# Cross attention on one Trainium2 core: the stabilizer's rows reach the query stack by transfers through DRAM instead of by turns on TensorE and copies

## What is computed

```
q, k, v = heads(x_q @ wq), heads(ctx @ wk), heads(ctx @ wv)
scores = q @ k.T / sqrt(16) + mask_or_relative_bias
probs = softmax(scores)            # over 4096 keys
out = probs @ v
```

## Time and profile before

| | us |
|---|---|
| three runs | 1622.54, 1625.29, 1626.94 |
| median | 1625.29 |
| the profiled execution | 1628.63 |
| its span, first to last instruction | 1626.8 |
| one head of cross attention, start to start | 11.1 |
| heads in all | 64 |

### The profile page before, as it was taken

How to read it: one execution, slowest core, us unless ns; L and a number is a source line. 1 busy time by engine, 2 the same in 40 slices (tenths; PEclk the granted TensorE clock), 3 DMA queues, 4 the chain that set the end, 5 groups by cost and what they waited for, 6 DMA issues and landing times. The chain is left out here.

```text
span 1626.8 us, 36711 instructions
## 1 busy us (share of the span) xinstructions
PE 1534.0 (94%) x12495; PEld 916.9 (56%) x12509; DVE 1057.2 (65%) x1619; ACT 874.6 (54%) x1910; POOL 338.7 (21%) x623
## 2 busy tenths in 40 slices
PE   9999998999999997998989999879999999989596
PEld 4444443444444444674868999724444444446396
DVE  6777788888888854748553111278888888726511
ACT  3222225888888883742632111238888888856232
POOL 1412221111111111020202444141111111100153
PEclk9999999999999999999989999999999999999799
DMA  6587763554554547100048999845545545222074
GB/s 213 178 209 233 217 177 82 90 90 77 90 88 77 91 93 183 35 1 1 2 146 272 327 315 318 262 80 95 93 78 87 89 79 88 48 24 83 29 231 131
DMA packets 158311, 207.46 MB, mean 128 GB/s; under 512 B 32135, under 2 KB 130434, under 8 KB 151158
## 3 DMA queue, kind: packets, MB, share of 16 engines
q1 hardware_dynamic: 149429, 199.99, 49.1%
q0 software_dynamic: 6720, 4.31, 1.6%
q10 hardware_dynamic: 2064, 1.87, 0.4%
HBM read 165.95 MB, written 41.39 MB: 127 GB/s over the span
## 5 line engine op out<-in xcount | busy, mean ns | idle before, releaser
L1339 DVE TENSOR_REDUCE top<-ps 128x1 f32<-128x1024 f32 x504 | 588.5, 1218 | 95.5 <-PE ps L1172 95.4
L1303 ACT ACTIVATE probs<-ps 128x512 f32<-128x512 f32 x1024 | 557.6, 601 | 132.1 <-PE ps L1204 121.4
L1204 PE MATMUL ps<-qst,kst 128*128 128x256 bf16 x2048 | 317.6, 276 | 4.8 <-ACT probs L1303 3.5
L1218 PE MATMUL ps_o<-probs,vst 128*32 128x256 f32 x4096 | 274.9, 386 | 1.4 <-ACT probs L1303 1.4
L1204 PEld LDWEIGHTS ps<-qst,kst 128*128 128x128 bf16 x2048 | 158.0, 98 | 205.8 <-ACT probs L1303 162.6
L1172 PE MATMUL ps<-kst,qst 64*128 64x512 bf16 (+1 forms) x519 | 170.6, 387 | 11.2 <-DVE top L1339 6.1
L1218 PEld LDWEIGHTS ps_o<-probs,vst 128*32 128x32 f32 x4096 | 107.0, 109 | 99.9 <-issue 41.5
L1172 PE MATMUL ps<-kst,q1st 64*128 64x512 bf16 x488 | 160.6, 386 | 0.0
L402 POOL COPY vst<-vall 128x512 f32 (+1 forms) x64 | 39.1, 611 | 555.3 <-PE ps_o L1218 552.2
L2437 PE MATMUL ps_h<-xe,vall 128*128 128x80 f32 x1024 | 149.7, 265 | 0.0
L2437 PEld LDWEIGHTS ps_h<-xe,vall 128*128 128x128 f32 x1024 | 136.3, 191 | 0.1
(11 more groups left out here) (458 smaller groups left out, 2126.7 us busy)
## 6 DMA issues: line engine op xcount, KB each, us to landing
kst<-kd SPq DMA_DIRECT2D x372, 128.0 KB
kd<-probs SPq DMA_DIRECT2D x64, 384.0 KB, 3.0
vall<-in_L_ffn_wg_dram SPq DMA_DIRECT2D x32, 512.0 KB
vall<-in_L_ffn_wu_dram SPq DMA_DIRECT2D x32, 512.0 KB
vall<-in_L_ffn_wd_dram SPq DMA_DIRECT2D x32, 512.0 KB
w<-in_L_ffn_w_dram SPq DMA_DIRECT2D x16, 1024.0 KB
vd<-square_weights SPq DMA_DIRECT2D x16, 512.0 KB, 4.1
vall<-vd SPq DMA_DIRECT2D x16, 512.0 KB, 6.5
```

Source lines behind the costliest of these rows:

```text
L1204: mm = pe.matmul(ps2[:, scores[u], x, :], kst[:, m, kt * P:(kt + 1) * P], qst[:, m, :], start=True, stop=True)
L1218: mm = pe.matmul(ps_o[32 * j:32 * j + 32, :], vst[:, b, kt, :], probs[:, (kt // 2) % SLOTS, kt % 2, :], start=(kt < 4), stop=(kt >= KT - 4 ...
L1303: nc.scalar.activation(probs[:, u % SLOTS, :, :], ps2[:, scores[u], :, :], ACT.Exp).then_inc(probs_ready, 1)
L1339: v.tensor_reduce(top[:, b, qt, c:c + 1], ps1[:, u % 2, :], AX, ALU.max).then_inc(mx, 1)
```

## The change

The columns of `cp` are no longer turned on TensorE, except for head 0 of each layer. For heads 1 to 31 SP stores the three columns, number by number (two transfers of 128 x 3 numbers of 2 bytes), as rows of a small DRAM tensor, waits until they have landed, and loads the three rows of 512 bytes into the query stack. GpSimd waits, before it overwrites `cp`, until the stores of the head before have landed. Unit 0 of pass 2 waits for the load (`c_in`). SP's list for head g becomes: second query rows, key rows, then the rows of head g - 2.

```diff
+    pr.c_dram = nc.dram_tensor("c_dram", [NBUF, NPIECE, S], BF16, kind="Internal").ap()
...
+        c_in = [pr.sem(st, f"c_in{m}") for m in range(NBUF)]
+        c_stored = [pr.sem(st, f"c_stored{m}") for m in range(NBUF)]
...
             def _(sp):
+                def turned_rows(n, m):
+
+                    wait_at(pr, sp, c_steps, C_STEPS * n)
+                    if not (isinstance(n, int) and n < FIRST):
+                        wait_at(pr, sp, q_ready, n + 1 - FIRST)
+                    else:
+                        sp.wait_ge(q_first[1], 2)
+                    for qt in range(QT):
+                        sp.dma_start(pr.c_dram[m, :, qt * P:(qt + 1) * P].rearrange("k p -> p k"), cp[:, qt, 0:NPIECE],
+                                     allow_slow_non_contiguous=True).then_inc(c_stored[m], 16)
+                    wait_at(pr, sp, c_stored[m], 8 * (n - m) + (32 if m >= 1 else 0))
+                    sp.dma_start(qst[CROW:CROW + NPIECE, m, :], pr.c_dram[m]).then_inc(c_in[m], 16)
...
                 for c in range(1, C):
                     sp.wait_ge(buffers.q_in[c], 16 * len(Q_ROWS))
+                turned_rows(1, 1)
                 with sp.Fori(1, NG // NBUF) as h2:
                     for m in range(NBUF):
                         g, h, _, b = head_number(h2, m)
                         wait_at(pr, sp, sc2, N2 * (g - NBUF + 1))
                         buffers.second_q(sp, h, m, b)
                         buffers.keys.load_k(sp, buffers.L, h, m)
+                        turned_rows(g - 2, (m + 2) % NBUF)
+                for m in range(2, NBUF):
+                    turned_rows(NG - NBUF + m, m)
...
-                def c_rows(n):
+                def c_rows(n, m):
 
                     pool.wait_ge(c_max, n)
+                    if not (isinstance(n, int) and n == 1):
+                        before = (m - 1) % NBUF
+                        pool.wait_ge(c_stored[before], 8 * (n - 1 - before) + (32 if before >= 1 else 0))
...
-                    if u == 0:
-                        pe.wait_ge(c_ready, g + 1)
+                    if u == 0 and first:
+                        pe.wait_ge(c_ready, 1)
+                    elif u == 0:
+                        pe.wait_ge(c_in[m], 4 * (g - m) + (16 if m >= 1 else 0))
                     if u == TURN_AT + 2 and not first:
                         pe.wait_ge(raw_ready, g)
-                    elif u == TURN_AT + 3 and not first and not last:
-                        pe.wait_ge(c_ready, g + 2)
...
-                        if u == (FIRST_TURN_AT if first else TURN_AT) and not last:
-                            turn_c(g + 1, place)
...
-                        if u == (FIRST_TURN_AT if place == "first" else TURN_AT) and place != "last":
-                            copy_c(g + 1, (m + 1) % NBUF, ps_first_c if place == "first" else ps_c)
```

More of the change, by code:

```diff
@@ L984, in cross_attention @@
     FIRST_SCORES2 = tuple((u + 2 * (u > FIRST_TURN_AT)) % 3 for u in range(N2))
-    F_SLOT, C_SLOT, FIRST_C_SLOT = (TURN_AT + 1) % 3, (TURN_AT + 2) % 3, (FIRST_TURN_AT + 2) % 3
+    F_SLOT, C_SLOT = (TURN_AT + 1) % 3, (TURN_AT + 2) % 3
     C_STEPS = 4
@@ L1000, in cross_attention @@
         ps_c = ps2[:, C_SLOT, 0, 0:P].bitcast(BF16)
-        ps_first_c = ps2[:, FIRST_C_SLOT, 0, 0:P].bitcast(BF16)
         ps_f = ps2[:, F_SLOT, 1, 0:QT * 64].rearrange("p (t d) -> p t d", t=QT)
@@ L1135, in _ @@
                 copy_first_v(1)
-                c_rows(1)
+                c_rows(1, 1)
                 for c in range(1, C):
@@ L1144, in _ @@
                         copy_q(g, h, m, m % 2)
-                        c_rows(g - 2)
+                        c_rows(g - 2, (m + 2) % NBUF)
                 for m in range(2, NBUF):
                     copy_v(*head_number(NG // NBUF - 1, m))
-                    c_rows(NG - NBUF + m)
+                    c_rows(NG - NBUF + m, m)
             @block.tensor
@@ L1174, in pass1, with turn_first_c @@
                     mm.then_inc(sc1, 1)
[L1176 to L1183, removed]
+                def turn_first_c():
+                    pe.wait_ge(c_first, CHAIN)
                     for qt in range(QT):
-                        mm = pe.transpose(turned[:, qt * P:(qt + 1) * P], cp[:, qt, :], pr.cb("identb"))
+                        mm = pe.transpose(ps_c[:, qt * P:(qt + 1) * P], cp[:, qt, :], pr.cb("identb"))
                     mm.then_inc(c_turned, 1)
                 def pass2(g, m, b, u, place):
-                    first, last = place == "first", place == "last"
+                    first = place == "first"
                     scores = FIRST_SCORES2 if first else SCORES2
-                    if u == 0:
-                        pe.wait_ge(c_ready, g + 1)
+                    if u == 0 and first:
+                        pe.wait_ge(c_ready, 1)
+                    elif u == 0:
+                        pe.wait_ge(c_in[m], 4 * (g - m) + (16 if m >= 1 else 0))
                     if u == TURN_AT + 2 and not first:
                         pe.wait_ge(raw_ready, g)
-                    elif u == TURN_AT + 3 and not first and not last:
-                        pe.wait_ge(c_ready, g + 2)
                     elif u == (FIRST_TURN_AT if first else TURN_AT) + 1:
@@ L1277, in _ @@
                     pe.wait_ge(q_read, C)
-                    turn_c(0, "before")
+                    turn_first_c()
                 else:
-                    turn_c(0, "before")
+                    turn_first_c()
                     for u in range(2):
@@ L1291, in copy_o, with copy_first_c @@
                     nc.scalar.copy(o_sb[:, b, :], ps_o).then_inc(o_copied, 1)
-                def copy_c(g, m, turned):
-                    act.wait_ge(c_turned, g + 1)
-                    nc.scalar.copy(qst[CROW:CROW + NPIECE, m, :], turned[0:NPIECE, :]).then_inc(c_ready, 1)
+                def copy_first_c():
+                    act.wait_ge(c_turned, 1)
+                    nc.scalar.copy(qst[CROW:CROW + NPIECE, 0, :], ps_c[0:NPIECE, :]).then_inc(c_ready, 1)
                 def head(g, h, m, b, place):
@@ L1327, in _ @@
                         act.wait_ge(buffers.k_out[q], 16 * NB)
-                copy_c(0, 0, ps_c)
+                copy_first_c()
                 all_heads(act, head)
```

## The result

The kernel after takes 2487.3 us, median of four runs (2482.81 to 2491.06); the kernel before took 1623.91 (1621.10 to 1626.94) beside it. The ratio is 1.532, 95% interval 1.530 to 1.535: 863 us more, where 36 were forecast and 1730 was the upper end of the range.

A forecast was written before the change was run, and what follows sets the result against it. TensorE, busy 94%, was taken to set the pace. Head stalls 30.8, less 4.8 gain, plus 7.9 in layer 1's head 1 and 2.0 for the clock: 35.9 us on 1625.3, forecast 1661, range 1622 to 1730.

The forecast's parts named there:

- the turns' 0.08 us per head: Unit 8 of a head, without turns: 0.08 of 0.20 us gained, 4.8 us over 60 places (0 to 12.0).
- T + 5.2: Issue of a head's first store, counted from T, when SP starts its work for a head; 5.2 us later.
- heads lose in pairs: Heads 2 to 29, both layers: two in a row lose 1.1 us together, 0.55 each, 30.8 us over 56.
- The chain as a whole: Stores, landing and row load before unit 0: rows land at T + 11.9, due at T + 10.8.
- where I had 2.0: Row load of three 512-byte rows: 2.0 us to land, the shortest landing shown; bounds 1.0 and 3.5.
- I take 1.0 us behind the key loads, T + 9.7: Stores' landing in each head: key loads end at T + 8.7, then 0.4 us of packets and 0.6 for landing.
- My upper bound, 3.5 us: Stores' landing at most 3.5 us behind the key loads, T + 12.2, taken from the mask's store.
- The third rival: Slow 2-byte stores in every head: rows at T + 13.5 to 14, +111 us, 1736 (1682 to 1790); chance 0.20.
- A head then takes 4.7 + (L - 5.2): For rows landing at T + L with a stall over 0.8 us, a head loses L - 11.6 against 11.1.
- I had allowed for it once, in layer 1: Lowered granted clock behind the stall at layer 1's head 1: 2 us added (0 to 4).
- Layer 1's head 1: SP waits there for the last query rows, so the stabilizer rows come 7.9 us late, once (6.3 to 10.9).
- its 2.0 + 2.0: Layer 1's head 1: 2.0 us for the stores' landing and 2.0 for the row load's.

The follow-up runs named there:

- the run with two hops: Changed kernel storing whole 64 bytes, then loading three rows of zeros from an input; stabilizer zero, exponential scale 0.1: 1664.2 us against 1622.2, ratio 1.026.
- the series: Landings of the store variants by writes into one 64 bytes, from 1.99 us (one whole 64-byte write) to 15.1 and 16.6 (32 writes).

## Why the prediction was wrong, point by point

**Right.** That TensorE sets the pace and that only the turns' 0.08 us per head come back: 4.1 (1.5 to 6.7) measured for 4.8. GpSimd's last step and SP's list as the two things that come before the store: T + 5.2 against T + 5.6 in the run with two hops. That key loads ahead of the stores delay their landing: with stores of 64 bytes it takes 10.4 - 5.6 = 4.8 us behind the key loads, and 2.0 with nothing ahead. That heads lose in pairs. The chain as a whole: +36 for +42 when the landing costs about what I had taken, with some luck: the row load was issued 0.5 us later than forecast, and from its issue to unit 0 it took 1.4 us where I had 2.0. About 48,000 more packets under 512 bytes: 81921 less 32135 on the page of before, 49,786.

**Wrong, and it decided: the step "I take 1.0 us behind the key loads, T + 9.7".** I put the landing together from 48 packets of 8.5 ns and 0.6 us. The packets do take that: the window from 714 to 716 shows 0.4 us of them. The landing, from the first issue, is 15.1 us in the median, and as long with nothing ahead in the queue. In layer 0's head 1 the window before the store shows the DMA engines at 0.00; SP's timeline stands under it:

```profile
264.00:265.80 1.80, 1.45 (x11) 0.49 (x10) 1.76 (x4) 1.57 (x3) 0.80 (x4) 1.00 0.00 0
```

```profile
265.83 0.92 SPq L1048 DMA_DIRECT2D c_dram<-cp  x2
281.35 0.26 SPq L1051 DMA_DIRECT2D qst<-c_dram  x1
```

My upper bound, 3.5 us, was taken from a store of the same number of pieces, but pieces of 128 bytes, each whole in itself. It was "the nearest row by its count of pieces", and the series says that the count of pieces is what doesn't matter. No row bounded what the change does: 2-byte writes side by side, 32 to each 64 bytes. The row load was priced too low as well, 3.0 us for 2.0; the load of three rows in the run with two hops took 1.4, and why the one from `c_dram` takes 1.6 more wasn't tried.

**The third rival** is the one that the result belongs to, by the sign set out for it, a head over 12.2 us with a late landing. It named the right fact, that many 2-byte stores go "to the same few hundred bytes, from all 16 engines", and priced it wrongly: 50 ns for each of 48 packets, 2.4 us, from which 1736 and at most 1790. Measured, 12.7 us are added to a landing (15.1 - 2.40). A price per packet was the wrong form: the packets are as short as ever, and 256 writes land no sooner than 768. The Trainium skill, DMA: Bandwidth & Descriptors, section Specifications, has the read-modify-write below 512 bytes as its rule. The runs bear on it from both sides: 768 writes of 2 bytes land in 2.40 us when apart, against 1.99 for 256 of 64 bytes, which are under 512 too, so being smaller still costs little; 32 of them in the same 64 bytes cost 15.1. That each must there read what the one before has left would explain both, but no run looked inside the memory.

**The formula for a large landing was right in form and lacked a term.** "A head then takes 4.7 + (L - 5.2)": landing and row load in it give 4.7 + 15.15 + 3.04 = 22.9 us; 24.9 were measured. The missing 2 us are the clock: I had allowed for it once, in layer 1, and not in a stalled head, since the heads were to stall by a microsecond. They stall by ten; the clock falls to 0.50 in each, and unit 0 to the end of GpSimd's last step takes 6.6 us for 4.6. At 0.8 and 0.99 us of stall, with the two hops, unit 0's matmuls keep their 0.39 us. With it the account closes: 62 heads wait for their rows; 62 x (22.9 - 11.1) = 732, 62 x 2.0 = 124, less 4 of gain, is 852 of the 863. Windows of the two cross attentions, in the columns of before:

```profile
252.00:1040.00 788.00, 422.39 (x3640) 175.44 (x3644) 298.52 (x299) 288.14 (x569) 53.21 (x184) 0.74 0.24 38
1495.00:2300.00 805.00, 426.97 (x3657) 177.88 (x3660) 305.93 (x304) 288.65 (x570) 63.24 (x199) 0.75 0.24 37
```

Before, these stretches lasted 364.5 and 368.0 us with PE busy for 358.4 and 358.7; PE's busy time grows by 64 and 68, with some hundred instructions fewer: the clock, which falls from 0.99 to 0.74 and 0.75.

**Layer 1's head 1**, forecast 7.9 us late (6.3 to 10.9): with the two hops its unit 0 has waited for 5.25 us, under my bounds; in the changed kernel 19.83 us. SP's timeline, then TensorE's, of the changed kernel:

```profile
1526.49 0.92 SPq L1048 DMA_DIRECT2D c_dram<-cp  x2
1541.13 0.27 SPq L1051 DMA_DIRECT2D qst<-c_dram  x1
```

```profile
1543.93 0.61 PE L1221 MATMUL ps<-qst,kst 128*128 128x256 bf16 x2 [19.83 <-DMA qst<-c_dram]
```

Store to row load 14.6, row load to unit 0 2.8: the terms of every other head. The place was right, its 2.0 + 2.0 were not.

**The chances.** I gave slower 0.70 and the slow stores 0.20 with an end at 1790. The direction held; the range ended where my price for a packet ended. The one thing that the trace could not price stood in the kernel's longest possible place, in front of every head, and I bounded it by rows that lacked its peculiarity.

**Open.** Whether the count of writes in 64 bytes decides or how many of the 16 engines meet there; what the unit is, between 16 and 512 bytes; whether single numbers into an SBUF row are slow as neighbours or for the one partition; what stops TensorE and ScalarE, beside the keys, while such stores are under way. A version that beats the kernel before isn't in sight of these runs: with the turns gone at no cost at all there were 4 us to win.

## What to carry to other kernels

A column that is to become a row through small transfers costs by its neighbours, not by its packets: when a store writes 2 bytes here and its neighbours go to the same 64 bytes, expect some 15 us from issue to landing, and other loads of the core held up meanwhile. Whole 64 bytes, or numbers spread apart, land in 2.0 to 2.5 us, but the single numbers then have to be gathered into the row, which took 8.2; no run here made the row cheaply. Two turns and a copy on engines with room are worth 0.07 us a head (4.1 us at 60 places), and a DRAM round trip in front of every head must fit into the slack of the chain or it is paid in full, with the clock on top. And when the trace lacks the operation itself, choose the nearest row by where its bytes go and not by their count, and leave the upper end open where none is near.

## What the runs showed of the hardware that I had not expected

- Stores whose packets are over by 716, with the DMA engines at 0.00 from there, land 12 us later. The packet rows don't show the price.
- 768 writes of 2 bytes: landing 2.40 us at 64 bytes' distance, 2.6 at 32, 4.35 at 8, 15.1 side by side. A write of 64 bytes in place of 32 writes of 2: 1.99.
- Such stores hold up others: with them TensorE waits 199 us for keys that it had not waited for before, and 198 when the stores stand in ScalarE's queue. Nobody waited for their data, and the kernel took 2123.6 and 2163.6 us; with the same stores apart, 1628.5.
- Into one SBUF row each, single numbers from DRAM take 8.2 us where they take 2.9 to 128 partitions; straight from SBUF's columns the way takes 10.7.
- One load of three such rows takes 11.0 us, three loads of one row each 8.2.
- Stalls of ten microseconds in every head cost another 2 us each through the granted clock, 0.50 for some 5 us after them; stalls of 0.8 to 1.0 us left unit 0's matmuls at their 0.39 us.
